# Attention scores in float32 on 32-row groups, maxima by the vector engine's fused pass, masks by a POOL select, gate rows by transfers

## What is computed

```
x = x + L0_attn(layernorm(x))           # linear attention: q,k l2-normed, 16 heads of 8
x = x + L0_ffn(layernorm(x))            # 8 experts (top 2 by softmax gate) + 2 shared:
                                        #   silu(x@w1)*(x@w3) @ w2, each expert times its gate
x = x + L1_attn(layernorm(x))           # 16 heads of 8:
                                        #   att = q@k.T / sqrt(8)
                                        #   att = -inf for every key after the query
                                        #   softmax(att) @ v @ Wo
x = x + L1_ffn(layernorm(x))            # 16 experts, each takes its best 512 tokens of 8192
```

## Time and profile before

| | |
|---|---|
| median of 3 runs | 2115.83 us (2112.31 to 2118.05) |
| the profiled execution, its own time | 2124.21 us |
| its span, first to last instruction | 2122.4 us |
| mean granted PE clock | 0.881 of full |
| busy: PE, DVE, ACT, POOL | 77%, 59%, 37%, 24% |
| the pipeline over the batches | from the start to about 1765 us |
| one pass of the loop | about 106.5 us |
| choice of tokens, then the experts of the second layer | about 155 us, then 202 us |

### The profile page before, as it was taken

How to read it: one execution, slowest core, us unless ns; L and a number is a source line. 1 busy time by engine, 2 the same in 40 slices (tenths; PEclk the granted TensorE clock), 3 DMA queues, 4 the chain that set the end, 5 groups by cost and what they waited for, 6 DMA issues and landing times.

```text
span 2122.4 us, 34602 instructions
## 1 busy us (share of the span) xinstructions
PE 1623.8 (77%) x10136; PEld 908.2 (43%) x10136; DVE 1243.4 (59%) x3733; ACT 793.3 (37%) x1515; POOL 502.1 (24%) x487
## 2 busy tenths in 40 slices
PE   3779888888888888888888888888899781137675
PEld 2345444444444444444444444444454441135554
DVE  5466757575757575757575757575766436861111
ACT  1225252525252525252525252525253342233331
POOL 2321212121212121212121212121212002007887
PEclk7879999989898989899999898999999875568888
DMA  2032231313131313131313031313031400023443
GB/s 64 19 46 41 31 53 24 52 24 58 18 56 20 58 18 58 18 54 22 56 19 59 17 59 17 56 20 59 17 56 21 65 7 10 0 35 84 90 92 59
DMA packets 113451, 86.62 MB, mean 41 GB/s; under 512 B 21440, under 2 KB 107840, under 8 KB 113344
## 3 DMA queue, kind: packets, MB, share of 16 engines
q1 hardware_dynamic: 102080, 76.64, 21.7%
q0 software_dynamic: 11264, 8.92, 3.0%
HBM read 59.02 MB, written 25.72 MB: 40 GB/s over the span
## 4 chain that ended last, share of the span: by engine, by line
PE 44%; issue 18%; DVE 17%; ACT 5%; POOL 5%; DMA 5%; SPq 2%; DVEq 1%; ACTq 0%; POOLq 0%
PE ba L579 6%; PE fa L668 5%; PE facc L694 5%; PE ba L584 4%; PE fa L684 4%; PE bo L838 4%; POOL out L551 3%; ACT probs L1017 2%; SPq L329 2%; DVE passed L1464 2%; PE ba L581 2%; PE ba L586 2%; DVE nm L1264 2%; DMA KT<-qk_parts 1%; POOL got L521 1%
## 5 line engine op out<-in xcount | busy, mean ns | idle before, releaser
L584 PE MATMUL ba<-KT,QT 72*128 72x512 bf16 (+3 forms) x1024 | 263.9, 321 | 188.5 <-DVE nm L1264 130.5
L1017 ACT ACTIVATE probs<-ba 128x512 f32<-128x512 f32 x640 | 330.3, 634 | 94.9 <-PE ba L581 94.0
L458 POOL TENSOR_TENSOR hh<-th,gb 128x512 f32<-128x512 f32 x128 | 162.1, 1267 | 713.5 <-ACT gb L970 437.2
L1264 DVE TENSOR_REDUCE nm<-ba 128x1 f32<-128x512 f32 x256 | 174.8, 683 | 191.7 <-issue 142.6
L579 PE MATMUL ba<-QT,KT 75*128 75x512 bf16 (+3 forms) x1024 | 254.8, 311 | 35.3 <-ACT probs L1017 28.9
L584 PEld LDWEIGHTS ba<-KT,QT 72*128 72x128 bf16 x1024 | 105.2, 103 | 350.2 <-DVE nm L1264 155.2
L586 PE MATMUL ba<-mask_q,identb 128*128 128x128 bf16 x1024 | 201.7, 231 | 0.0
L581 PE MATMUL ba<-mask_k,identb 128*128 128x128 bf16 x1024 | 197.1, 225 | 0.0
L668 PE MATMUL fa<-f_nT,w 128*128 128x512 f32 x320 | 187.1, 669 | 2.3 <-ACT sc L1048 1.2
L684 PE MATMUL fa<-f_nT,w 128*128 128x512 f32 x320 | 181.0, 649 | 0.0
L986 ACT ACTIVATE sil<-fa 128x512 f32<-128x512 f32 x160 | 95.1, 594 | 213.8 <-PE fa L668 213.6
(11 more groups left out here) (283 smaller groups left out, 2681.2 us busy)
## 6 DMA issues: line engine op xcount, KB each, us to landing
QT<-qk_parts SPq DMA_DIRECT2D x288, 64.0 KB
KT<-qk_parts SPq DMA_DIRECT2D x288, 64.0 KB
qk_parts<-qkp SPq DMA_DIRECT2D x32, 384.0 KB, 2.5
fc<-in_L_ffn_fc_weight SPq DMA_DIRECT2D x32, 256.0 KB, 2.9
xin<-in_L_attn_x SPq DMA_DIRECT2D x16, 256.0 KB, 14.3
out<-x SPq DMA_DIRECT2D x16, 256.0 KB, 2.3
xn_rows<-row SPq DMA_DIRECT2D x16, 256.0 KB, 2.4
w<-in_L_w SPq DMA_DIRECT2D x3, 640.0 KB, 6.9
```

The source lines that it names most:

```text
L458: pool.tensor_tensor(hh[:, e % 2], th[:, e % 2], gb[:, e % 2], ALU.mult).then_inc(S["s_h"], 1)
L584: pe.matmul(bank[:, col:col + w], lhsT=QT[0:QK_ROWS, head, blk * P:(blk + 1) * P], rhs=KT[0:QK_ROWS, head, 0:w], start=True, stop=False)
L1017: act.activation(probs[:, pair % 3, f_], ba[n % 3][:], ACT.Exp, scale=SCALE).then_inc(S["s_exp"], 1)
L1264: last = dve.tensor_reduce(nm[:, 3, h:h + 1], bank[:], X, ALU.max, negate=True)
```

## The change

- Scores are computed in float32, without parts: the contraction of a head has 8 rows (9 with the maxima). Head 4v + g lies at rows 32g of QT and KT, turn v; a **burst** computes the strips of four heads (g = 0 to 3) into four banks ba0 to ba3, each from its own 32-row group of PE's array. A phase has ten bursts: four "long" (one strip of 512), four "mixed" (384 and 128) and two "half" (two strips of 256). Each bank is single: a burst waits, bank by bank, for the reader of the burst before.
- The mask matmuls are gone. By query, DVE adds a mask table and takes the maximum in one instruction (`tensor_tensor_reduce`), which also writes the masked scores back to the bank. By key, the masked exponentials are set to zero by a POOL select (`cut`), for which `outputs` now waits.
- The parts of q, k and the maxima are gone, with their ACT, DVE and POOL instructions, and `gate_rows` with ACT's copies. The gates are transposed by DVE in 32x32 blocks, written to DRAM by 4 transfers and read back by 8 transfers of 256 KB that spread each row over 128 partitions (`gate_dmas`), at the end of SP's pass.
- The shared experts come first (ORDER). The back transfers of q and k are 8 for each half, of 32 KB.

```diff
+BURSTS = [("long", 0), ("mixed", 0), ("half", 0), ("long", 1), ("mixed", 1),
+          ("long", 2), ("mixed", 2), ("half", 2), ("long", 3), ("mixed", 3)]
...
+ORDER = [E0, E0 + 1] + list(range(E0))
...
+            def gate_dmas(b):
+
+                sp.wait_ge(S["s_gtr"], b + 1)
+                apart(sp)
+                for i in range(P // 32):
+                    sp.dma_start(gate_rows[b].rearrange("e (q i r) -> i (e q) r", i=P // 32, r=32)[i], gates_t[32 * i:32 * i + 32]).then_inc(S["s_gw"], 16)
+                sp.wait_ge(S["s_gw"], 16 * (P // 32) * b + 16 * (P // 32))
+                apart(sp)
+                sp.wait_ge(S["s_h"], E0 * b)
+                apart(sp)
+                for e in range(E0):
+                    sp.dma_start(gb[:, e], gate_rows[b, e].partition_broadcast(P)).then_inc(S["s_gb0" if e < 2 else "s_gb1"], 16)
...
                 part_dmas(i + 1)
                 both(back_dmas, i + 1)
+                gate_dmas(i + 2)
...
+            def cut(b, n):
+
+
+                for g in range(GROUPS):
+                    pool.wait_ge(S["s_exp"], BANKS * b + n * GROUPS + g + 1)
+                    apart(pool)
+                    blocks = probs[:, n % UNIT, g].rearrange("p (m k) -> p m k", k=P)
+                    blocks = blocks[:, {"long": slice(0, 1), "mixed": slice(0, 4, 3), "half": slice(0, 3, 2)}[BURSTS[n][0]]]
+                    pool.affine_select(blocks, blocks, [[0, blocks.shape[1]], [1, P]], ALU.is_ge, 0.0, base=0, channel_multiplier=-1)\
+                        .then_inc(S["s_cut"], 1)
...
+                todo = pieces(n, by_key)
+                for i, (v, blk, col) in enumerate(todo):
+                    for g in range(GROUPS):
+                        if n > 0 and i == 0:
+                            pe.wait_ge(S["s_exp" if by_key else "s_red"], BANKS * b + (n - 1) * GROUPS + g + 1)
+                        own, rows = slice(blk * P, (blk + 1) * P), slice(g * ROWS, g * ROWS + HD + (1 if by_key else 0))
...
+                            mm = pe.matmul(ba[g][:, col:col + (blk + 1) * P], lhsT=QT[rows, v, own], rhs=KT[rows, v, 0:(blk + 1) * P],
+                                           start=True, stop=True)
...
+                for j in range(U0):
+                    if b is not None:
+                        burst(b, j, False)
+                    if f is not None and j + 1 < U0:
+                        up(f, j + 1)
+                        up3(f, j + 1)
...
+                    pe.wait_ge(S["s_cut"], BANKS * b + [3, 5, 8, 10][k] * GROUPS)
...
+                dve.wait_ge(S["s_S"], len(BURSTS) * b + n + 1)
+                apart(dve)
+                for g in range(GROUPS):
+                    for v, blk, col in pieces(n, False):
+                        w, h = (blk + 1) * P, v * GROUPS + g
+                        last = dve.tensor_tensor_reduce(ba[g][:, col:col + w], ba[g][:, col:col + w], mask_q[:, SEQ - w:], -1.0, -MASKED,
+                                                        ALU.add, ALU.min, nm[:, blk, h:h + 1])
+                    last.then_inc(S["s_red"], 1)
...
-            dve.memset(KT[64:96], 1.0).then_inc(S["s_pad"], 1)
+            dve.memset(KT[:], 1.0).then_inc(S["s_pad"], 1)
```

More of the change, by code:

```diff
@@ L258, in bcast_rows @@
             return v.rearrange("(o n) -> o n", o=1)[0].partition_broadcast(P)
-        first, beside = 3, [4] * (U0 - 2) + [3, 2]
-        assert first + sum(beside) == FILLS
-        fills_of = [range(first + sum(beside[:e]), first + sum(beside[:e + 1])) for e in range(U0)]
         def looped(engine, x_phase, y_phase):
@@ L589, in prob_block, with pieces @@
-        def prob_block(h, blk):
-            slot, k = (h // 2) % 3, h % 2
-            if blk == 0:
-                return probs[:, slot, 2 * k, :]
-            if blk == 1:
-                return probs[:, slot, 2 * k + 1, 0:384]
-            if blk == 3:
-                return probs[:, slot, 2 * k + 1, 384:512]
-            return probs[:, slot, 4, 256 * k:256 * k + 256]
+        def pieces(n, by_key):
+            kind, v = BURSTS[n]
+            if kind == "long":
+                return [(v, 0 if by_key else 3, 0)]
+            if kind == "mixed":
+                return [(v, 1, 0), (v, 3, 384)] if by_key else [(v, 2, 0), (v, 0, 384)]
+            return [(v, 2, 0), (v + 1, 2, 256)] if by_key else [(v, 1, 0), (v + 1, 1, 256)]
@@ L640, in f_out @@
                 for q in range(Q):
-                    last = pe.matmul(fa[2][:, q * D:(q + 1) * D], lhsT=qnT[:, q * P:(q + 1) * P], rhs=kvo[:], start=True, stop=True)
+                    last = pe.matmul(fa[1][:, q * D:(q + 1) * D], lhsT=qnT[:, q * P:(q + 1) * P], rhs=kvo[:], start=True, stop=True)
                 last.then_inc(S["s_at0"], 1)
@@ L686, in down, with up @@
[L686 to L691 removed]
+            def up(b, j):
+                if j == 0:
+                    pe.wait_ge(S["s_nT2"], b + 1)
+                else:
+                    pe.wait_ge(S["s_sil"], U0 * b + j)
+                pe.matmul(fa[0][:], lhsT=w1[:, ORDER[j]], rhs=f_nT[:], start=True, stop=True).then_inc(S["s_h1"], 1)
@@ new lines, in up3, with down @@
+            def up3(b, j):
+                if j == 0:
+                    pe.wait_ge(S["s_lge"], b + 1)
+                elif j <= SHARED:
+                    pe.wait_ge(S["s_hs"], SHARED * b + j)
+                else:
+                    pe.wait_ge(S["s_t"], E0 * b + j - SHARED)
+                pe.matmul(fa[1][:], lhsT=w3[:, ORDER[j]], rhs=f_nT[:], start=True, stop=True).then_inc(S["s_h3"], 1)
+            def down(b, j):
+                if j < SHARED:
+                    pe.wait_ge(S["s_hs"], SHARED * b + j + 1)
+                else:
+                    pe.wait_ge(S["s_h"], E0 * b + j - SHARED + 1)
+                if j == 0:
@@ L749, in turn_maxima @@
+            def turn_maxima(b, half):
+                pe.wait_ge(S["s_red"], BANKS * b + (half + 1) * BANKS // 2)
+                pe.wait_ge(S["s_x3" if half == 0 else "s_l1c"], b)
                 for q in range(Q):
-                    last = pe.transpose(bo[:].bitcast(BF16)[0:PARTS * HEADS // 2, q * P:(q + 1) * P],
-                                        nmp[:, half, q].rearrange("p c h -> p (c h)"), identb[:])
+                    last = pe.matmul(bo[0:HEADS // 2, q * P:(q + 1) * P], lhsT=nm[:, q, half * HEADS // 2:(half + 1) * HEADS // 2], rhs=ident[:],
+                                     start=True, stop=True)
@@ L802, in x_phase @@
-                if b is not None:
-                    turn_maxima(b, 0)
+                for j in range(U0):
+                    if b is not None:
+                        burst(b, j, False)
+                    if f is not None and j + 1 < U0:
+                        up(f, j + 1)
+                        up3(f, j + 1)
+                    if t is not None and j == 8 and b is not None:
+                        pe.wait_ge(S["s_nmT"], 2 * b + 1)
+                    if t is not None and j in T_STEPS:
+                        T_STEPS[j](t)
+                    if b is not None and j == 6:
+                        turn_maxima(b, 0)
+                    if f is not None and j > 0:
+                        down(f, j - 1)
@@ L905, in across @@
                 pe.wait_ge(S[ready], n)
-                pe.matmul(fa[2][:, col:col + src.shape[-1]], lhsT=pattern[:], rhs=src[:], start=True, stop=True).then_inc(S[done], 1)
+                pe.matmul(facc[:, col:col + src.shape[-1]], lhsT=pattern[:], rhs=src[:], start=True, stop=True).then_inc(S[done], 1)
             for i in range(8):
@@ L1270, in maxima @@
-                last.then_inc(S["s_red"], 1)
+                dve.wait_ge(S["s_S"], len(BURSTS) * b + n + 1)
+                apart(dve)
+                for g in range(GROUPS):
+                    for v, blk, col in pieces(n, False):
[3 more added lines that the diff above has]
+                    last.then_inc(S["s_red"], 1)
```

538 lines of the change are left out of this document (200 added, 338 removed).

## The result

The changed kernel takes 2213.77 us (median of 4 runs, 2212.84 to 2215.4) against 2116.94 of the kernel before in the same job: a ratio of 1.0473 [1.0438, 1.0509], 4.7% slower. The forecast of 2037 us is 177 us too low and has the wrong sign. The profiled execution of after took 2212.84 us, its span is 2211.1, its granted PE clock 0.808 of full, where before had 0.881.

What follows compares the result with a forecast made beforehand. Bound by DVE's stall at the jump, DVE's maxima in the X phase, then ACT and PE together. Twelve passes with a jump -88 us, four without +13, start -4: -79 from 2115.8 gives 2037 us; range 1940 to 2164.

Steps and rivals of the forecast that it cites:

- A after: From the last gate step across the loop's jump to DVE's first maxima: 3.0 us instead of 13.6, -10.6.
- the stall stays: Rival, chance 0.22: DVE's fetch behind the jump still takes its 13.6 us; kernel 2164 us.
- The maxima: DVE's masked maxima in the X phase: 0.67 us per strip of 512; ten bursts 30.0 us against 25.2.
- The bursts: PE's four-head score strips overlap: a long burst 1.0 us, a mixed or half one 1.7 for 16 loads.
- row groups do not overlap: Rival, chance 0.10: PE's row groups run serially (0.04, 2485 us) or in pairs (0.06, 2117 us).
- B after: From DVE's first maxima behind the jump to the addition closing the X phase: 50.6 us from 48.9, +1.7.
- The wait for the input: At step 2 of the X phase DVE waits for `load_x`, queued behind the gate rows: +1.5 us (0 to 4).
- C after: From the addition closing the X phase to the gates' end: walk of 44.2 us against 44.0; in all +1.6.
- POOL's select: Masking of by-key exponentials: some 0.65 us for 256 columns, four ending 1.4 us behind the last exponential.
- POOL binds: Rival, chance 0.08: selects of 1 us and more hold up the by-key phase, +4.4 us a batch, 2107 us.
- The drain: Behind the last X-phase addition, where the pipeline empties: not examined; priced as a pass without a jump, +3.
- by twos: Rival case, chance 0.06: PE's row groups overlap only in pairs, bursts of 1.9 us, about +5 a batch, 2117 us.

Runs made afterwards that it cites:

- experiment 2: The changed kernel with by-key strips contracting all 32 rows of their group instead of 9, the added rows zero in QT: 2098.45 us, ratio 0.9939.
- experiment 5: The changed kernel without POOL's selects, outputs waiting for the exponentials themselves (mask by key left out): 2203.18 us, ratio 1.04.

## Why the prediction was wrong

- **A after: right in kind, 1.7 us short.** 4.7 us for 3.0 (-8.9 where -10.6 was forecast); DVE stands 4.0 us behind the jump where the forecast's sign was "near 3". The rival *the stall stays* fell. That the stall was DVE's fetch behind the transfers was an inference; moving the transfers in the kernel before confirms the transfers. That it is instructions which wait there rests on the word "issue" and the place at the jump; no row names the fetch.
- **The maxima: right in kind, a little dear.** A strip of 512 starts 0.65 us after the one before (0.67), a mixed bank 0.77 (0.80), 256 columns 0.38 (0.40). No half rate for the write into the bank.
- **The bursts: dear.** Mixed and half bursts take 1.1 us as long ones do, not 1.7: the 16 records of a half burst are through in 1.08 (986.80 to 987.88), where 16 loads at 0.10 would take 1.6, so the loads of four groups overlap. (Waits for their banks make many of them longer, and so does the half clock: 2.0 for the long burst at 932.02.) A long burst of the changed kernel's B takes 1.07 (991.54 to 992.61) where four serial strips would take 4 x 0.91, a factor of 3.4. The rival *row groups do not overlap* fell.
- **B after: near, 52.0 for 50.6.** The wait for the input, +1.5 us in the sum, did not come. It pays some 3 us for a stretch at 0.50 behind the jump (978.7 to 985.3, after PE had stood still for 2.3 us), and gets part of them back in cheaper bursts and maxima.
- **C after: the failed step.** The walk of it holds within 0.7 us, at full clock. In the fastest pass of experiment 2, from 972.7: outputs at 14.1, 21.1, 30.1 and 39.3 us (forecast 14.1, 21.6, 30.8, 39.3), the exponentials of bursts 4 and 9 end at 19.6 and 38.7 (19.5, 38.6), C 44.1 (44.2). The step assumed every price at full clock and never asked what the new strips do to the clock; its bounds, -3 and +6, held no term for it. In the changed kernel the same outputs start at 16.6, 24.3, 33.3 and 46.6, the clock is 0.77, and C is 52.5: 6.9 us over the forecast, 12 times 83 us. Strips of 32 rows in place of 9 bring C back to 45.6.
- **POOL's select: dear.** 0.375 us on average over both widths, where 0.65 was taken for 256 columns; one comes every 0.49 us, with the exponentials. At full clock outputs 2 and 3 start 0.6 us behind their last exponential, not 1.4, so the 1.4 us that the sum added to the walk of 44.2 did not come. That the mean C of experiment 2 still is 45.6 is the clock, at 0.93 to 0.96 in most passes: two small errors cancel there, by luck. POOL is not in the path while the clock is down (experiment 5). The rival *POOL binds* fell.
- **The drain: missed.** The forecast gave the last batch the price of a pass without a jump. It is 40.8 us longer. By-key strips of few rows account for 11 of these, by experiment 2; the rest, in which the bursts run alone and mostly at 0.50, as the strips of the kernel before did in part, stays open.
- **Sum.** A pass with a jump is over the forecast by 1.7 (A), 1.4 (B) and 6.9 (C), 10.0, and by 0.7 more since the pass it was read from was longer than the mean of 105.8: 12 times that are 129 us. The last pass is over by 9 and the drain by 38, the first two passes under by 9, the start by 1. Together they make up the 167 us between the forecast's -79 and the +88.7 of the spans, within a rounding; the forecast of 2037 is 177 us off, since it was taken from the median. So the step in C is half of the miss, and the drain under a quarter.

No rival named the clock. The nearest, *by twos* at 2117, would have given a slower PE by a mechanism that the traces do not show. The range's upper end of 2164 held one mishap, the return of the stall, but not a common factor on every matmul of C.

## What to carry to other kernels

Packing small contractions into row groups of PE buys concurrency (a long burst of four strips in 1.07 us, for 3.64 one after another), but with strips that fill few of their rows the granted clock was lower here (0.77 in C for 9 rows, 0.93 to 1.00 for 32): pad the contraction with rows of zeros to the full 32, which cost no time (a long burst of 32 rows took 1.07 us too) and gave back some 5% in float32 (2214 to 2098), with both phases 6% (2080). In bfloat16 it gave under 2% (2009 to 1980). Price a change at the clock that it will be granted, and look apart at the stretch where a pipeline runs empty. Keep matmuls over the whole array out from between the strips of a burst (1.7 us each here). And before a loop's jump look at what the DMA queues still hold: moving 18 transfers behind it made the old kernel 4.9% faster, which beats the change and its repaired forms in float32 (2011 against 2080 us). A list of waits can hide such a stall under the name of an engine that was long done.
